# TensorE's stages written out in another order, example by example; the orders of the other engines, buffers and waits unchanged

## The reference

```python
# L0 fuse: attention over 64 memory rows per example, then a gate
mem = ctx @ W_mem.T ; ctx0 = softmax(x @ mem.T) @ mem
x = rmsnorm(x + sigmoid([x, ctx0] @ W_gate.T + b) * ctx0)      # in essence
# L1 and L3, the same block with different weights and token types
h = rms_norm(x); q, k, v = where(expert, h @ v_qkv, h @ l_qkv)  # 16 heads of 16, rotary, causal
x = x + where(expert, att @ v_dense, att @ l_dense)
x = x + cross_attention(rms_norm(x), ctx) @ cdense_w            # 16 heads of 8, 64 keys
m = rms_norm(x)
x = x + where(expert, silu(m@v_gate)*(m@v_up)@v_down, silu(m@l_gate)*(m@l_up)@l_down)
# L2: gated attention over the 64 media rows (16 heads of 64), then a gelu block of 1024
x = x + tanh(g1) * attention(layernorm(x) @ Wq, media @ Wkv) @ Wo
x = x + tanh(g2) * gelu(layernorm(x) @ W1) @ W2
```

## Time and profile before

| | |
|---|---|
| median of 3 runs | 1384.2 us (1384.14 to 1384.94) |
| span of the profiled execution | 1380.9 us |
| TensorE (PE) busy | 1306.9 us, 95% |
| VectorE (DVE) busy | 764.5 us, 55% |
| ScalarE (ACT) busy | 473.6 us, 34% |
| GpSimd (POOL) busy | 452.1 us, 33% |

### The profile page before, as it was taken

One profiled execution on the slowest core, in us unless ns is written; L12 is line 12 of the kernel. 1 busy time (PEld: TensorE's weight loads), 2 busy tenths in 40 slices (PEclk: granted clock), 3 DMA queues, 4 the chain that ended last, 5 costly groups with the idle time before them and its releaser, 6 DMA issues.

```text
span 1380.9 us, 25903 instructions
## 1 busy us (share of the span) xinstructions
PE 1306.9 (95%) x10931; PEld 1047.3 (76%) x10931; DVE 764.5 (55%) x1361; ACT 473.6 (34%) x785; POOL 452.1 (33%) x559
## 2 busy tenths in 40 slices
...
DMA packets 19901, 27.29 MB, mean 20 GB/s; under 512 B 3432, under 2 KB 15552, under 8 KB 19520
## 3 DMA queue, kind: packets, MB, share of 16 engines
...
## 4 chain that ended last, share of the span: by engine, by line
PE 84%; DVE 6%; ACT 5%; POOL 3%; issue 2%; ACTq 0%; DVEq 0%; POOLq 0%
PE bank L1433 6%; PE bank L1723 6%; PE bank L1688 5%; PE bank L1693 5%; PE bank L1577 5%; PE bank L1933 4%; PE bank L1940 4%; PE bank L1897 4%; PE row_banks L1527 4%; PE row_banks L1837 3%; PE row_banks L1560 3%; PE bank L1495 3%; PE bank L1712 3%; PE bank L1426 3%; PE row_banks L1532 2%; ACT room L2051 2%
## 5 line engine op out<-in xcount | busy, mean ns | idle before, releaser
L1283 POOL TENSOR_SCALAR_AFFINE_SELECT room<-room 128x1024 f32<-128x1024 f32 x64 | 70.7, 1107 | 185.3 <-ACT room L2051 185.3
L2293 DVE TENSOR_REDUCE room<-row_banks 128x4 f32<-128x512 f32 (+1 forms) x128 | 116.4, 952 | 23.1 <-PE row_banks L1532 22.8
L2051 ACT ACTIVATE room<-row_banks 128x1536 f32<-128x1536 f32 x64 | 92.9, 1451 | 90.0 <-PE row_banks L1560 90.0
L1723 PE MATMUL bank<-room,down_w 128*128 128x256 f32 x384 | 95.9, 391 | 0.5 <-DVE room L2393 0.5
L2307 DVE RECIPROCAL room<-bank 128x256 f32<-128x256 f32 x32 | 56.1, 1754 | 59.3 <-PE bank L1577 59.3
L2083 ACT ACTIVATE room<-bank 128x256 f32<-128x256 f32 x96 | 36.4, 383 | 148.6 <-PE bank L1693 137.6
L1245 POOL TENSOR_TENSOR room<-room 128x256 f32<-128x256 f32 x32 | 24.5, 767 | 173.0 <-ACT room L2063 173.0
L1723 PEld LDWEIGHTS bank<-room,down_w 128*128 128x128 f32 x384 | 70.4, 192 | 14.0 <-issue 4.9
L1357 POOL TENSOR_TENSOR room<-room 128x512 f32<-128x512 f32 x32 | 33.7, 1070 | 133.1 <-DVE room L2495 132.9
L1560 PE MATMUL row_banks<-room 32*128 32x256 f32 (+1 forms) x1024 | 62.1, 357 | 9.7 <-ACT room L2051 4.6
L1560 PEld LDWEIGHTS row_banks<-room 32*128 32x128 f32 x1024 | 48.9, 190 | 27.6 <-issue 15.6
...
## 6 DMA issues: line engine op xcount, KB each, us to landing
...
```

Of the source, the lines that this page charges most:

```text
L1283: pool.affine_select(out=diagonal, in_=diagonal, compare_op=ALU.is_ge, fill=0.0, base=0, pattern=[[0, 8], [1, P]], channel_multiplier=-1)\
L1723: return pe.matmul(ff_bank[0][:, t * S:(t + 1) * S], down_w[:, f, t * P:(t + 1) * P], hid[:, i, :], start=(i == t == 0), stop=(i == UPS - ...
L2051: act.activation(probs[w % 2], row_banks[:, :, 0:3 * P], ACT.Exp).then_inc(*ATT_ACT.does(e, f"exp{w}"))
L2293: last = dve.tensor_reduce(dst, row_banks[:, :, P * i:P + S * i], X, ALU.max, negate=True)
```

## The change

The number tables and the sort go. In their place stands `ORDER`, one text for each engine with its stages in order, and `whole_order()` splits the texts into words. From `walk` on the two programs are the same text, so every stage has the same instructions, waits and buffers; a line number of the changed kernel is that of before less 477. The lists of ScalarE, VectorE, GpSimd and the DMA queue come out exactly as before. TensorE's list has the same 1150 stages, and 485 of them stand at another place, in 133 separate pieces from the first to the last example, mostly moved by 1 to 8 places; the furthest are `b_project.0.0` (23 places earlier), `.0.1` (22), `f_mem.0.3` (12) and `memory.8` (10).

```diff
-    put(1545.6724, "f_scores")
-    put(1546.6753, "f_turn")
...
-FUSE_STARTS = [3049.804, 3050.034, 3050.465, 3050.769, 3059.408, 3059.728, 3060.114, 3060.433]
...
+ORDER = {
+    "pe": """
+        x_turn.0 x_turn.1 x_turn.2 x_turn.3 x_turn.4 p_vec.0 f_scores.0 f_mem.0.0 x_turn.5 x_turn.6 f_scores.1
+        x_turn.7 f_scores.2 f_turn.0 f_turn.1 p_trig.0 f_scores.3 f_context.0 f_turn.2 f_mem.0.1 f_context.1 f_turn.3
+        f_mem.0.3 f_gate.0 f_context.2 f_context.3 f_gate.1 f_gate.3 f_gate.2 f_sum.0 f_mem.0.2 f_sum.1 f_spread.0
...
 def whole_order():
 
-    order = [(time, stage, 0, *which) for time, stage, *which in once_stages()]
...
+    order = []
+    for stages in ORDER.values():
+        for word in stages.split():
+            stage, *at = word.split(".")
+            order.append((stage, *map(int, at)))
+    return order
```

More of the change, by code:

```diff
@@ L210, in norm_stages @@
[L210 to L253, removed]
@@ L256, in project_stages @@
[L256 to L316, removed]
-        put(-795.5664, "v_out")
-        put(-773.2386, "k_mask")
-        put(-760.2458, "q_mask")
-        put(678.2822, "q")
-        put(679.6758, "k")
-        put(681.0539, "v")
-    return at
@@ L736, in late_stages @@
-def late_stages(layer):
-    at = []
-    def put(time, stage, *which):
-        at.append((time, stage, *which))
-    if layer == 0:
-        put(-795.0729, "late_hidden", 0)
-        put(-789.7925, "late_hidden", 1)
-        put(-787.5722, "late_hidden", 2)
-        put(-768.1993, "late_give")
-        put(-396.2381, "late_tanh", 0)
-        put(-389.6257, "late_tanh", 1)
-        put(-388.9090, "late_tanh", 2)
-        put(1075.8038, "late_up", 0)
-        put(1085.0578, "late_up", 1)
-        put(1087.6136, "late_up", 2)
-        put(1091.4216, "late_down", 0)
-        put(1091.5721, "late_down", 1)
-        put(1091.6445, "late_down", 2)
-    else:
-        put(-820.9191, "late_hidden", 0)
-        put(-816.4043, "late_hidden", 1)
-        put(-805.9962, "late_hidden", 2)
-        put(-793.2257, "late_give")
-        put(-411.8007, "late_tanh", 0)
-        put(-408.5689, "late_tanh", 1)
-        put(-408.2277, "late_tanh", 2)
-        put(1067.5916, "late_up", 0)
-        put(1071.5727, "late_up", 1)
-        put(1093.9126, "late_up", 2)
-        put(1100.5828, "late_down", 0)
-        put(1100.9230, "late_down", 1)
-        put(1101.1351, "late_down", 2)
-    return at
```

892 lines of the change are left out of this document (323 added, 569 removed).

## The result

The changed kernel takes 1391.05 us (median of 4 runs, 1390.34 to 1392.61) against 1384.32 for the kernel before on the same chip: ratio 1.0048, 95% interval 1.0034 to 1.0062. It is slower by 6.7 us where 4.6 us of gain were forecast. Its profiled execution has a span of 1389.3 us and took 1391.21 us.

The account below looks back on a forecast made before the run. TensorE, busy 1306.9 of 1380.9 us, was taken as the bound, leaving 74 us idle to change. Terms +6.0 - 0.3 - 0.5 - 1.3 - 4.2 - 0 - 2.5 - 1.0 - 0.8 = -4.6 gave 1379.6 us, range 1373 to 1387.

Parts of the forecast that it names:

- Fuse, examples 0 to 3: a loss of about 6.0 us: First fuse half: 4.5 us of new TensorE waits plus 1.5 us longer tail; bounds 4 to 7 us.
- Rival D: Idle between 22 and 35 us halves the clock and the gates run at it: 1386.7 up to 1394 us; chance 0.16.
- `f_mem` is only work moved: First fuse half: f_gate.0 is 4.5 us later, with f_turn.3 and f_mem.0.3 already done.
- The signs named ahead: Wrong if clock under 1.00 in 20-60 us, f_scores.4 under 4 us late, or middles' idle up over 2 us.
- 182 to 505: Stretch of 182 to 505 us: four stages put into waits gain 1.3 us; bounds 0 to 3.6.
- Rival B: The fuse's loss is smaller by 2 to 4 us and the gains hold: 1373 to 1377 us; chance 0.15.
- Rival C: Downstream gains are taken back by the next release: 1384.9 us, range 1381.4 to 1387; chance 0.27.
- 505 to 592: Stretch of 505 to 592 us: up.7.0 2.4 us earlier with 1.73 us done ahead, gain 4.2; bounds 2.4 to 6.6.
- 592 to 895: Stretch of 592 to 895 us, 49 pieces: gain 0, at most 1.75 us to be had; bounds -1 to +3.
- 895 to 970: Stretch of 895 to 970 us: first_scores.9.3 fills the wait of crs_spread.8.0, among others; gain 2.5 us, bounds 1.5 to 3.
- 1006 to 1310: Stretch of 1006 to 1310 us: values.14 and turn_max.14 go into waits; gain 1.0 us, bounds 0 to 1.5.
- The end: Program end: down.14.0 goes into the 2.34 us wait ahead of cross_project.15; gain 0.8 us, bounds 0.5 to 1.7.

Follow-up runs that it names:

- e3: Changed kernel with f_turn.3 and f_mem.0.3 moved behind f_gate.0: 1387.39 us, ratio 1.0028 to the kernel before.
- e14: Kernel before with only f_mem.0.3 moved behind f_turn.3 and f_mem.0.2 ahead of f_sum.1: 1390.78 us, ratio 1.0051.
- e15: Kernel before with only the gates in the order 0, 1, 3, 2: 1393.44 us, ratio 1.0068.

## Why the prediction was wrong

**The step that failed** is the largest term, "Fuse, examples 0 to 3: a loss of about 6.0 us". It was summed from waits and from durations at full clock, and the fuse costs 15.2 us instead of the 5.7 of both halves together. Its waits were right: 0.89, 0.60 and 2.00 us for 1.1, 0.8 and 2.1. Missing are the matmuls that run at half clock behind them. From `f_turn.3` to the second quarter of `f_gate.0` (33.71 to 37.33) they take 3.62 us, against 2.18 for the same work at full clock: 1.4 us. With the tail, 2.1 us longer for the 1.5 forecast, `f_scores.4` is 8.2 us late for 6.0. Behind it, `f_turn.6` and `f_gate.4` have changed places and are taken together: from `f_scores.4` to the end of both it is 19.3 us for 12.3 before, another 7.0 lost at half clock. That makes 15.2 us; by `n0_sum.0` it is 14.4.

**Rival D** was the case that came, with 0.16. Its time, 1386.7 to 1394, holds the measured 1391.05, and that is luck in part, since it priced other matmuls than those that ran slow. It had the mechanism right and the place wrong: it let the gates run at half, but these ran at full from 37 us on, and the long stretch fell on the scores and turns of the second half, behind thin stages, not behind the wait that I had priced. By the Trainium skill, "TensorE: Matmul & The Clock Gate", section "HAM oscillation — how this bites in real kernels", the matmuls behind a wait run at the lower clock at first, a cost on top of the wait. The traces agree: the stretch at half clock behind the wait of 2.00 us goes with it (run e3, 2.6 us less), and the parts tried in e14 and e15 cost 7.6 and 10.3 us, where `f_scores.4` comes 0.5 us later and a chain of 1.5 to 2.1 us is added. The first 20 us at 1.00 with 12 of 20 us busy, which I held against it, said nothing about the middle of the program.

**"`f_mem` is only work moved"** was the second error in that step. I counted `f_mem.0.3`, done early, as paid back. In its old place it stood among the thin stages, and the two `f_mem` moved alone cost 7.6 us.

**The signs named ahead.** The granted clock did fall under 1.00 between 20 and 60 us, and that was the sign that mattered. `f_scores.4` was 8.2 us late, so not under 4. Idle time in 182 to 505 us went up by 2.6 us (323 less 316.75, against 3.6), which was named as a sign too; but the stretch now begins with work that stood ahead of 182 before. Between the same stages, `dense.1` and `dense.7`, idle time fell from 4.9 to 4.4 us.

**Rival B** (the loss is smaller) is excluded. **Rival C** (the gains are taken back) is excluded for the later parts as a whole: forecast 10.3 us (0.5 + 1.3 + 4.2 + 2.5 + 1.0 + 0.8), measured 10.5 with the old fuse. That the sum fits so well is luck in part, since single terms below are off by 1 to 2 us each way.

**The terms.** 505 to 592: forecast 4.2, alone 3.7. (`a_sum.0` stands 5 places earlier in TensorE's list, not the 7 that the working has, and `b_project.0.2` and `.0.3` have come forward by 16 and 15 places too, which it leaves out.) 592 to 895: forecast 0, alone 1.6. 895 to 970: forecast 2.5, with the old fuse 3.0 (10.5 less 7.5, by intervals that meet), with the new one none that can be told. 182 to 505: forecast 1.3, by the trace of the changed kernel 0 (13.9 us late at its start, 14.2 at its end): the waits named go, but `first_scores.5.2` gets a new one of 0.86 us and `cross_values.5` one of 0.56. The wait at 164 us gave 0.3 of 0.5. 1006 to 1310: forecast 1.0, by the trace 2.6 (`cross_first.9` 10.5 us late, `cross_first.14` 7.9). The end: forecast 0.8, by the trace a loss of 0.5 (`dense.15` 7.7 us late, `up.15.0` 8.2). The second half of the fuse: forecast 0.3, by the trace about 0.4 (15.2 us late behind `f_gate.4`, 14.8 at `f_sum.4`). Of the terms, the second half of the fuse, the two ahead of 505 us and the two behind 1006 us were not tried alone.

**Left open.** Why five of six runs of one kernel lose some 10 us at a low clock and one does not is not settled by these runs; only that the time follows the mean clock. Nor is it settled what in the thin stages brings the fall, the width of the matmuls or how long TensorE is busy. Whether the later gains are smaller behind the new fuse is not settled either: the difference of 2 us lies inside the intervals.
